# A sandwich of attention and routed low-rank layer: another order of VectorE's work in the middle of a pass

## The chip, the cores and the metric

The kernel runs on one core of one Trainium2 chip. The metric is the device time of one execution in microseconds (us); before the change it is 150.67 us, the median of 3 runs (150.66 to 150.72).

## What is computed

The input x has 16 sequences of 256 rows of 128 numbers, all fp32. Two residual sub-layers follow each other, each as x + layernorm(f(layernorm(x))):

```
def reference(x, ...):
    x = x + layernorm(attention(layernorm(x)))
    x = x + layernorm(ffn(layernorm(x)))

attention: 2 heads of 64; the upper 32 of each head's q and k are rotated (rotary angles);
           softmax(q k^T / 8) v, then the output projection Wo
ffn:       base = x W^T
           p = l2norm(x Wp^T + bp); logits = p @ l2norm(sim) * exp(min(temp, log 100))
           lw = softmax(logits); only the top expert of a row keeps its weight
           result = base + sum over experts e of lw_e * (x Wd_e^T) Wu_e^T,  ranks 1, 2, 4, 8
```

## The kernel before

**Tiling and stages.** The 16 sequences are worked as 8 pairs. A pair has 4 tiles of 128 rows (two per sequence) and 4 units (sequence b, head h: unit u = 2b + h). The kernel is one software pipeline written out by hand: the loop `for a in PASSES` (a = 0 to 6) stands once on each of four engines, and in pass a each engine does its share for several pairs at once: the attention of pair a, the projection of q, k and v of pair a + 1, the statistics of the first layernorm of pair a + 3, the residual after attention and its statistics for pair a - 1, and routing, gates and the final residual of pair a - 2. Pair 7 and the rest of pairs 5 and 6 are done after the loop in a written-out tail. Every engine executes its instructions in the order of the text; semaphores say when a value of another engine (or a small one of its own) is there. Nothing plans this order but the text.

**TensorE (PE), in one pass:** transposes of q and k (`turn_qk`, L1341), `project_qkv` (L1329 to L1331), transposes of the probabilities (`turn_probs`, L1362) and products with v (`weigh`, L1372) for units 0 to 3, `scores` (L1352), transposes of the gates (`turn_gated`, L1403), `low_rank` (L1410), and late in the pass `turn_x2` (L1383: transposes of the residual x after attention; it waits for all four tiles of `residual_y`), `turn_probs` of unit 3, `turn_qk` and `weigh` of unit 2, `project_z` (L1395), `turn_x` (L1322: transposes of the normalised x of pair a + 2, for which `normalise` of ACT and of DVE must be done).

**ScalarE (ACT):** the exponentials `exps` (L438, waits for the row maximum), copies from PSUM (`probs_copy`, `qk_copy`, `v_copy`, `qkt_copy`, `x2_copy`, `rows_up`, `gated_copy`), the sums of squares `variance_y` (L449) and `variance_z` (L474), half of `normalise` (L415) and `expert_exps` (L463, the exponentials of the routing, which wait for `logits`).

**GpSimd (POOL):** powers of four values per partition (`inverse_lengths` L293, `factors_y` L297, `norm_rows` L266, `factors_z` L305, `deviation` L309), and the rotation of q and k, `rope` (L282, L285, L288), three operations on 256 elements per partition with two SBUF inputs each, twice in a pass.

**VectorE (DVE)**, whose order the change rewrites: `row_max` (L675, negated row maxima of a unit's scores, read from PSUM); `weights_sum` and `add_head` (L680, L688); the first layernorm's statistics of pair a + 3: `stats` (L643, four times), `gap` (L649, L650), `mean` (L654, L655), `variance` (L659); the residual `residual_y` (L695, one tile each; inputs y_all and x_all, both in SBUF), its statistics `stats_2`, `gap_2`, `square_2`, `variance_2`; the routing chain `keys`, `top_key`, `logits`, `is_top`, `shares`, `pick`, `sum_exps`, `invert_sum`, `gates`, `gates_low` (L750 to L794), at whose end stands `gated`, which `turn_gated` transposes; `residual_z` (L799); `normalise` for tiles 0 and 1 of pair a + 2 (L664, SBUF to SBUF).

`logits` reads `below` and so far needs no wait of its own for it, as `keys`, which waits for it, stands in front. Passes 2, 3 and 4 have every part; pass 0 has no pair a - 1 or a - 2 and pass 1 no pair a - 2; in passes 5 and 6 there is no pair a + 3, so no `stats`, `gap`, `mean` or `variance`.

Of the kernel before, what the change touches and what calls it, by code (L numbers as in the profile page):

```python
# [43 lines left out]
def layer(nc, x, w_attn, vectors, w_ffn, w_down, sim, out):  # L44
# [3 lines left out]
    with ctx:  # L48
# [144 lines left out]
        def has(n):  # L193
            return 0 <= n < PAIRS
# [194 lines left out]
        def _(act):  # L389
# [56 lines left out]
            def variance_y(n, b):  # L446
                act.wait_ge(y_ready, n * 4 + 2 * b + 2)
                for t in (2 * b, 2 * b + 1):
                    last = act.activation(sq_y[:, t, :], y_all[:, n * PT + t, :], ACT.Square, scale=E ** -0.5,  # L449
                                          accum_out=var_y[:, t:t + 1])  # L450
                last.then_inc(vary, 1)
# [9 lines left out]
            def expert_exps(n):  # L461
                act.wait_ge(logits_ready, n + 1)
                act.activation(expl[:, :, :], logit[:, :, :], ACT.Exp).then_inc(exps_ready, 1)  # L463
# [62 lines left out]
            for a in PASSES:  # L526
                now, nxt, done = has(a), has(a + 1), has(a - 2)
                if done:
                    squares(a - 2)
                if now:  # L530
                    exps(a, 0)
                if a == 0:
                    rows_up(1)
                    v_first(0)
                    v_first(1)
                if now:
                    qkt_copy(a, 1)
                if has(a - 1):
                    variance_y(a - 1, 1)
                if now:  # L540
                    exps(a, 1)
                if done:
                    expert_exps(a - 2)
                if now:
                    probs_copy(a, 0)
                if nxt:
                    qk_copy(a + 1, 0)
                    v_copy(a + 1, 0)
                    qk_copy(a + 1, 1)
                    v_copy(a + 1, 1)  # L550
                    qk_copy(a + 1, 2)
                if now:
                    probs_copy(a, 1)
                if done:
                    gated_copy(a - 2)
                if nxt:
                    v_copy(a + 1, 2)
                if now:
                    exps(a, 2)
                if done:  # L560
                    variance_z(a - 2)
                if now:
                    exps(a, 3)
                if nxt:
                    qk_copy(a + 1, 3)
                if now:
                    probs_copy(a, 2)
                if has(a - 1):
                    x2_copy(a - 1)
                if has(a + 2):  # L570
                    act.wait_ge(rstd1, a + 1)
                    normalise(a + 2)
                if now:
                    variance_y(a, 0)
                if nxt:
                    qkt_copy(a + 1, 0)
                if now:
                    probs_copy(a, 3)
                if has(a + 2):
                    rows_up(a + 2)  # L580
                if nxt:
                    v_copy(a + 1, 3)
# [34 lines left out]
        def _(dve):  # L617
# [112 lines left out]
            def rank_wide(row):  # L730
                return row[:, :].unsqueeze(2).to_broadcast([P, PT, RANK])
# [18 lines left out]
            def keys(n):  # L750
                dve.wait_ge(route_link, n * 9 + 3)
                dve.scalar_tensor_tensor(key[:, :, :], below[:, :, :], 0.0,
                                         code[:, :].unsqueeze(1).to_broadcast([P, PT, RANK]), ALU.is_ge, ALU.mult).then_inc(route_link, 1)
# [4 lines left out]

            def logits(n):
                dve.wait_ge(inv_norm_ready, n + 1)  # L760
                dve.tensor_tensor(logit[:, :, :], below[:, :, :], rank_wide(inv_norm), ALU.mult).then_inc(logits_ready, 1)

            def is_top(n):
# [304 lines left out]
            for a in PASSES:  # L1068
                now, nxt, far, last_, done = has(a), has(a + 1), has(a + 2), has(a - 1), has(a - 2)
                if done:  # L1070
                    add_bias(a - 2, 1)
                if nxt and a >= 1:
                    rows_low(a + 1)
                if done:
                    top_logit(a - 2)
                    square_sum(a - 2)
                if now:
                    row_max(a, 0)
                if done:
                    length(a - 2)  # L1080
                if last_:
                    weights_sum(a - 1, 3)
                if done:
                    below_top(a - 2)
                if last_:
                    add_head(a - 1, 3, 0)
                    add_head(a - 1, 3, 1)
                if now:
                    row_max(a, 1)
                if a == 0:  # L1090
                    rows_low(1)
                    centre_bias()
                    later_weights(1)
                    for t in range(PT):
                        stats(2, t)
                    gap(2)
                    mean(2)
                    variance(2)
                if a == 1:
                    later_weights(5)  # L1100
                if done:
                    keys(a - 2)
                if has(a + 3):
                    stats(a + 3, 0)
                if done:
                    top_key(a - 2)
                    logits(a - 2)
                    is_top(a - 2)
                if has(a + 3):
                    stats(a + 3, 1)  # L1110
                    stats(a + 3, 2)
                if done:
                    shares(a - 2)
                    pick(a - 2)
                if has(a + 3):
                    stats(a + 3, 3)
                if done:
                    sum_exps(a - 2)
                if last_:
                    residual_y(a - 1, 0)  # L1120
                if done:
                    invert_sum(a - 2)
                if has(a + 3):
                    gap(a + 3)
                if done:
                    gates(a - 2)
                if has(a + 3):
                    mean(a + 3)
                if done:
                    gates_low(a - 2)  # L1130
                if has(a + 3):
                    variance(a + 3)
                if now:
                    row_max(a, 2)
                if last_:
                    residual_y(a - 1, 1)
                    residual_y(a - 1, 2)
                if now:
                    row_max(a, 3)
                    weights_sum(a, 0)  # L1140
                if a == 0:
                    later_weights(3)
                if last_:
                    stats_2(a - 1, 0)
                if now:
                    add_head(a, 0, 0)
                if last_:
                    stats_2(a - 1, 1)
                if now:
                    add_head(a, 0, 1)  # L1150
                if last_:
                    residual_y(a - 1, 3)
                    stats_2(a - 1, 2)
                    stats_2(a - 1, 3)
                if now:
                    weights_sum(a, 1)
                if last_:
                    gap_2(a - 1)
                if now:
                    add_head(a, 1, 0)  # L1160
                if last_:
                    square_2(a - 1)
                if now:
                    add_head(a, 1, 1)
                if last_:
                    variance_2(a - 1)
                if done:
                    residual_z(a - 2, 0)
                    residual_z(a - 2, 1)
                if far:  # L1170
                    normalise(a + 2)
                if done:
                    residual_z(a - 2, 2)
                    residual_z(a - 2, 3)
                if now:
                    weights_sum(a, 2)
                if a == 0:
                    later_weights(2)
                if last_:
                    scaled_bias(a - 1)  # L1180
                if now:
                    add_head(a, 2, 0)
                if last_:
                    add_bias(a - 1, 0)
                if now:
                    add_head(a, 2, 1)
                if a == 0:
                    later_weights(4)
# [436 lines left out]
```

## Time and profile before

| what | us |
|---|---|
| median of 3 runs | 150.67 |
| the profiled execution | 150.58 |
| its span in the profile | 148.8 |
| PE busy | 128.5 (86%) |
| DVE busy | 130.7 (88%) |
| ACT busy | 113.4 (76%) |
| POOL busy | 87.3 (59%) |

The profiled execution's own time is 1.8 us above its span (start and end outside of the profile) and 0.09 us below the median. "Busy" is the share of the span in which an engine had an instruction under way. The granted TensorE clock is 9 tenths or more of full speed in 37 of the 40 slices of the page and lower only in the last three, after the loop. Line numbers (L654) are those of the kernel before. In the lists over time, an instruction's duration runs from its start to its end, and the next one on the same engine may start some 0.08 us before that end; in the chain of waits each piece is counted from the end of the piece before it.

### The profile page before, as it was taken

The page shows a single profiled execution, that of the slowest core. Times are in us where ns is not written, and L with a number is a line of the kernel's source. Part 1 is how long each engine was busy: PE and PEld are TensorE (multiplying, and loading weights), DVE is VectorE, ACT ScalarE, POOL GpSimd, SP SyncE. Part 2 cuts the span into 40 slices and gives each one's busy share as a digit, 9 for nine tenths or more (in the row PEclk, how much of TensorE's full clock was granted, in tenths as well). Part 3 has the DMA queues.
Part 4 walks back from the last instruction along what each step waited for, and adds up shares of the span by engine and source line. Part 5 has one row for each costly group of instructions (what it writes and reads, how often), then busy time and mean ns, then how long its engine had stood idle before and what let it go on. Part 6 is the DMA issues. An engine that isn't in the chain of part 4 may idle for free.

```text
span 148.8 us, 3110 instructions
## 1 busy us (share of the span) xinstructions
PE 128.5 (86%) x874; PEld 106.0 (71%) x874; DVE 130.7 (88%) x592; ACT 113.4 (76%) x378; POOL 87.3 (59%) x148
## 2 busy tenths in 40 slices
PE   0879799999999998999899989998999898965340
PEld 0467587988898788878887888797879776953220
DVE  6788879997988999899989998898889788899963
ACT  3657697969996989698969896989698958754460
POOL 6320826623846758676867686768545863338552
PEclk9999999999999999999999999999999999999555
DMA  3833250000000000100020002000200010000013
GB/s 74 209 98 92 74 134 5 4 0 0 7 0 2 0 0 4 70 0 2 4 73 0 0 0 75 0 0 0 73 4 2 9 62 0 4 0 2 0 70 141
DMA packets 5266, 4.83 MB, mean 32 GB/s; under 512 B 594, under 2 KB 5250, under 8 KB 5250
## 3 DMA queue, kind: packets, MB, share of 16 engines
q1 hardware_dynamic: 5104, 4.51, 10.4%
q8 instruction: 7, 0.11, 0.3%
q10 hardware_dynamic: 146, 0.13, 0.3%
q14 instruction: 9, 0.07, 0.2%
HBM read 2.54 MB, written 2.10 MB: 31 GB/s over the span
## 4 chain that ended last, share of the span: by engine, by line
PE 49%; DVE 27%; ACT 15%; issue 2%; POOL 2%; DMA 2%; POOLq 1%; DVEq 0%
PE ps_a L1372 6%; PE ps_s L1352 6%; ACT probs L438 6%; PE ps_z L1395 5%; PE ps_c L1372 4%; DVE neg_max L675 4%; PE ps_a L1362 4%; DVE x_all L695 3%; PE ps_b L1322 2%; PE ps_s L1383 2%; PE ps_s L1341 2%; PE ps_b L1362 2%; DVE y_all L688 2%; DMA x_all<-x 2%; PE ps_c L1341 2%
## 5 line engine op out<-in xcount | busy, mean ns | idle before, releaser
L438 ACT ACTIVATE probs<-ps_s,neg_max 128x256 f32<-128x256 f32 x60 | 25.3, 488 | 7.9 <-DVE neg_max L675 7.8
L675 DVE TENSOR_REDUCE neg_max<-ps_s 128x2 f32<-128x512 f32 x30 | 20.3, 680 | 0.6 <-PE ps_s L1352 0.4
L1352 PE MATMUL ps_s<-qk_t 64*128 64x256 f32 x120 | 17.0, 402 | 0.0
L1372 PE MATMUL ps_a<-v_all,probs_t 128*128 128x129 f32 x120 | 16.5, 280 | 0.0
L1372 PEld LDWEIGHTS ps_a<-v_all,probs_t 128*128 128x128 f32 x120 | 14.6, 191 | 2.0 <-issue 2.0
L1352 PEld LDWEIGHTS ps_s<-qk_t 64*128 64x128 f32 x120 | 10.3, 186 | 4.8 <-issue 4.0
L282 POOL TENSOR_TENSOR turn<-qk,sin_x 128x256 f32<-128x256 f32 x15 | 11.1, 740 | 3.1 <-ACT qk L424 2.2
L695 DVE SCALAR_TENSOR_TENSOR x_all<-y_all,rsy,x_all 128x128 f32<-128x128 f32 x32 | 11.8, 393 | 1.3 <-POOL rsy L297 0.7
L285 POOL TENSOR_TENSOR qk<-qk,cos_x 128x256 f32<-128x256 f32 x15 | 11.5, 767 | 1.2
L297 POOL TENSOR_TENSOR rsy<-var_y,power 128x4 f32<-128x4 f32 x6 | 6.5, 1078 | 9.3 <-ACT sq_y L449 9.3
L293 POOL TENSOR_TENSOR inv_norm<-norm,power 128x4 f32<-128x4 f32 x7 | 7.2, 1027 | 8.0 <-DVE norm L744 8.0
L288 POOL TENSOR_TENSOR qk<-qk,turn 128x256 f32<-128x256 f32 x15 | 10.9, 725 | 1.2
L266 POOL TENSOR_TENSOR rs<-ve,power 128x4 f32<-128x4 f32 x7 | 7.1, 1008 | 6.2 <-DVE ve L659 6.2
L449 ACT ACTIVATE sq_y<-y_all 128x129 f32<-128x129 f32 x32 | 10.1, 339 | 0.7 <-DVE y_all L688 0.6
L309 POOL TENSOR_TENSOR std<-ve,root 128x4 f32<-128x4 f32 x7 | 7.1, 1017 | 5.3 <-DVE ve L716 5.3
L1362 PE MATMUL ps_a<-ident,probs 128*128 128x128 f32 x60 | 9.1, 275 | 1.1 <-ACT probs L438 1.1
L444 ACT ACTIVATE probs_t<-ps_a 128x512 f32<-128x512 f32 x15 | 9.5, 637 | 0.5 <-PE ps_a L1362 0.5
L1395 PE MATMUL ps_z<-w_z,x_t 128*128 128x190 f32 x48 | 9.5, 325 | 0.0
L1362 PEld LDWEIGHTS ps_a<-ident,probs 128*128 128x128 f32 x60 | 7.0, 140 | 2.6 <-ACT probs L438 1.6
L1372 PE MATMUL ps_c<-v_all,probs_t 128*128 128x129 f32 x64 | 8.6, 278 | 0.2 <-ACT probs_t L444 0.2
L799 DVE SCALAR_TENSOR_TENSOR x_all<-ps_z,rsz,x_all 128x128 f32<-128x128 f32 x24 | 7.3, 342 | 1.4 <-POOL rsz L305 1.4
L1372 PE MATMUL ps_b<-v_all,probs_t 128*128 128x129 f32 x64 | 8.5, 276 | 0.0
(342 smaller groups left out, 442.0 us busy)
## 6 DMA issues: line engine op xcount, KB each, us to landing
x_all<-x SPq DMA_DIRECT2D x7, 256.0 KB, 2.8
out<-x_all SPq DMA_DIRECT2D x7, 256.0 KB, 2.1
x_all<-x SPq DMA_DIRECT2D x2, 128.0 KB, 2.7
out<-x_all SPq DMA_DIRECT2D x2, 128.0 KB, 1.7
w_raw<-w_attn ACTq DMA_DIRECT2D x1, 128.0 KB, 2.8
w_raw<-w_attn SPq DMA_DIRECT2D x1, 128.0 KB, 2.9
bo_bp<-vectors SPq DMA_DIRECT2D x1, 80.0 KB, 3.5
ffn_raw<-w_ffn SPq DMA_DIRECT2D x1, 71.5 KB
```

The costliest lines, as they stand in the source:

```text
L282: pool.tensor_tensor(turn[:, b, :, :, :], swapped, sin_x[:, :, :, :, :].rearrange("p t g h i -> p (t g) h i"), ALU.mult).then_inc(rope_mid, 1)
L285: pool.tensor_tensor(spatial, spatial, cos_x[:, :, :, :, :].rearrange("p t g h i -> p (t g) (h i)"), ALU.mult).then_inc(rope_mid, 1)
L288: pool.tensor_tensor(spatial, spatial, turn[:, b, :, :, :].rearrange("p g h i -> p g (h i)"), ALU.add).then_inc(rope_done, 1)
L438: last = act.activation(probs[:, u, j, :], scores_of(n, u)[:, j * T:(j + 1) * T], ACT.Exp, bias=neg_max[:, u, j:j + 1])
L444: act.activation(probs_t[:, u, :, :], unit_of(n, u)[:, :].rearrange("p (a t) -> p a t", a=TILES), ACT.Copy).then_inc(pt_out, 1)
L449: last = act.activation(sq_y[:, t, :], y_all[:, n * PT + t, :], ACT.Square, scale=E ** -0.5, accum_out=var_y[:, t:t + 1])
L675: dve.tensor_reduce(neg_max[:, u, :], scores_of(n, u)[:, :].rearrange("p (j k) -> p j k", j=TILES), AX.X, ALU.max, negate=True).then_inc(m ...
L695: dve.scalar_tensor_tensor(x_all[:, rows(n, t)], y_all[:, n * PT + t, 0:E], rsy[:, t:t + 1], x_all[:, rows(n, t)], ALU.mult, ALU.add).then ...
L1352: last = pe.matmul(scores_of(n, 2 * b + h)[:, j * T:(j + 1) * T], qk_t[r, b, 0, j * P:(j + 1) * P], qk_t[r, b, 1, :], start=True, stop=True)
L1362: last = pe.transpose(unit_of(n, u)[:, i * T + j * P:i * T + (j + 1) * P], probs[:, u, j, i * P:(i + 1) * P], ident[:, :])
L1372: last = pe.matmul(unit_of(n, u)[:, j * VW:(j + 1) * VW], probs_t[:, u, i, j * P:(j + 1) * P], v_all[:, at:at + VW], start=(i == 0), stop= ...
L1395: last = pe.matmul(z_of(n, k)[:, t, :], x2_t[:, 2 * k + t, :], w_z[:, :], start=(t == 0), stop=False, skip_group_check=True)
```

## The change

On DVE, `logits` moves in front of `keys` and gets a wait of its own for `below`. The four `stats` are spread otherwise between the parts of the routing chain, and the routing chain runs to its end (`gates_low`) with `residual_y` of tile 0 and `gap` in between. `mean` and `variance` leave the middle of the pass and stand behind `variance_2`, in front of `residual_z`. `residual_y` of tile 3 moves from behind `add_head(a, 0, 1)` to directly behind tiles 1 and 2, in front of `row_max(a, 3)`. On ACT, `expert_exps` moves in front of `exps(a, 1)`. PE, POOL and the DMA queues keep their order, and no instruction is added or removed besides the one wait.

```diff
--- before.py
+++ after.py
@@ -537,10 +537,10 @@
                     qkt_copy(a, 1)
                 if has(a - 1):
                     variance_y(a - 1, 1)
+                if done:
+                    expert_exps(a - 2)
                 if now:
                     exps(a, 1)
-                if done:
-                    expert_exps(a - 2)
                 if now:
                     probs_copy(a, 0)
                 if nxt:
@@ -758,6 +758,7 @@
 
             def logits(n):
                 dve.wait_ge(inv_norm_ready, n + 1)
+                dve.wait_ge(route_link, n * 9 + 3)
                 dve.tensor_tensor(logit[:, :, :], below[:, :, :], rank_wide(inv_norm), ALU.mult).then_inc(logits_ready, 1)
 
             def is_top(n):
@@ -1099,42 +1100,40 @@
                 if a == 1:
                     later_weights(5)
                 if done:
+                    logits(a - 2)
                     keys(a - 2)
                 if has(a + 3):
                     stats(a + 3, 0)
                 if done:
                     top_key(a - 2)
-                    logits(a - 2)
-                    is_top(a - 2)
                 if has(a + 3):
                     stats(a + 3, 1)
+                if done:
+                    is_top(a - 2)
+                    shares(a - 2)
+                if has(a + 3):
                     stats(a + 3, 2)
                 if done:
-                    shares(a - 2)
                     pick(a - 2)
+                    sum_exps(a - 2)
                 if has(a + 3):
                     stats(a + 3, 3)
                 if done:
-                    sum_exps(a - 2)
+                    invert_sum(a - 2)
                 if last_:
                     residual_y(a - 1, 0)
                 if done:
-                    invert_sum(a - 2)
+                    gates(a - 2)
                 if has(a + 3):
                     gap(a + 3)
                 if done:
-                    gates(a - 2)
-                if has(a + 3):
-                    mean(a + 3)
-                if done:
                     gates_low(a - 2)
-                if has(a + 3):
-                    variance(a + 3)
                 if now:
                     row_max(a, 2)
                 if last_:
                     residual_y(a - 1, 1)
                     residual_y(a - 1, 2)
+                    residual_y(a - 1, 3)
                 if now:
                     row_max(a, 3)
                     weights_sum(a, 0)
@@ -1149,7 +1148,6 @@
                 if now:
                     add_head(a, 0, 1)
                 if last_:
-                    residual_y(a - 1, 3)
                     stats_2(a - 1, 2)
                     stats_2(a - 1, 3)
                 if now:
@@ -1164,6 +1162,9 @@
                     add_head(a, 1, 1)
                 if last_:
                     variance_2(a - 1)
+                if has(a + 3):
+                    mean(a + 3)
+                    variance(a + 3)
                 if done:
                     residual_z(a - 2, 0)
                     residual_z(a - 2, 1)
```

## Rows read from the trace of the kernel before

**Rows 1.** Busy time by window; one window is one pass; us, then each engine's.

```profile
60.41:75.32 14.91, 14.30 (x106) 12.18 (x105) 14.43 (x62) 12.96 (x46) 10.62 (x17) 1.00 0.06 19
90.22:105.06 14.84, 14.29 (x106) 12.17 (x105) 12.85 (x53) 12.90 (x46) 10.80 (x17) 1.00 0.06 22
31.27:45.49 14.22, 14.19 (x103) 12.08 (x102) 12.62 (x50) 12.19 (x37) 7.12 (x11) 1.00 0.01 2
```

**Rows 2.** Chain of waits in pass 3: start, length, what.

```profile
71.24 0.66 PE ps_s L1383 x4
71.89 0.44 PE ps_a L1362 x4
```

**Rows 3.** DVE over time in pass 3, and L654 over the run (min/median/max).

```profile
66.62 0.73 DVE L654 SCALAR_TENSOR_TENSOR mean<-tmp,stats 128x4 f32<-128x4 f32 x1
67.47 0.69 DVE L659 SCALAR_TENSOR_TENSOR ve<-tmp 128x4 f32<-128x4 f32 x1
...
L654 DVE SCALAR_TENSOR_TENSOR mean<-tmp,stats x7: 165/168/726, 14.3 to 81.5; 128x4 f32<-128x4 f32 x7
```

**Rows 4.** POOL over time in pass 3.

```profile
66.59 0.74 POOL L282 TENSOR_TENSOR turn<-qk,sin_x 128x256 f32<-128x256 f32 x1
67.40 0.74 POOL L285 TENSOR_TENSOR qk<-qk,cos_x 128x256 f32<-128x256 f32 x1
```

**Rows 5.** Chain of waits in pass 5: start, length, what.

```profile
98.21 0.38 ACT gated_t L467
...
101.41 0.66 PE ps_a L1362 x4
```

**Rows 6.** ACT over time in pass 3.

```profile
64.21 0.84 ACT L438 ACTIVATE probs<-ps_s,neg_max 128x256 f32<-128x256 f32 x2
64.93 0.27 ACT L463 ACTIVATE expl<-logit 128x60 f32<-128x60 f32 x1
...
70.65 0.89 ACT L438 ACTIVATE probs<-ps_s,neg_max 128x256 f32<-128x256 f32 x2
```

**Rows 7.** PE's weight loads over time in pass 3.

```profile
65.52 0.73 PEld L1352 LDWEIGHTS ps_s<-qk_t 64*128 64x128 f32 x8 [0.36 <-issue]
```

**Rows 8.** DVE over time in pass 0.

```profile
26.58 0.16 DVE L680 RECIPROCAL den<-ps_a 128x2 f32<-128x2 f32 x1
...
28.66 1.38 DVE L664 TENSOR_SCALAR xn<-x_all,rs,nm 128x128 f32<-128x128 f32 x2
```

**Rows 9.** POOL over time in pass 0.

```profile
28.41 0.74 POOL L282 TENSOR_TENSOR turn<-qk,sin_x 128x256 f32<-128x256 f32 x1 [1.09 <-ACT qk L424]
...
30.04 0.72 POOL L288 TENSOR_TENSOR qk<-qk,turn 128x256 f32<-128x256 f32 x1
```

**Rows 10.** Chain of waits in passes 0 and 1: start, length, what.

```profile
25.43 0.89 PE ps_a L1372 x8
...
30.75 0.59 PE ps_b L1322 x4
...
41.41 0.66 PE ps_s L1383 x4
```

**Rows 11.** ACT over time in pass 1.

```profile
35.60 0.84 ACT L438 ACTIVATE probs<-ps_s,neg_max 128x256 f32<-128x256 f32 x2
```

**Rows 12.** PE over time in pass 1.

```profile
36.68 1.13 PE L1352 MATMUL ps_s<-qk_t 64*128 64x256 f32 x8
```

**Rows 13.** DVE over time in pass 1.

```profile
37.84 0.69 DVE L675 TENSOR_REDUCE neg_max<-ps_s 128x2 f32<-128x512 f32 x1
38.45 1.08 DVE L695 SCALAR_TENSOR_TENSOR x_all<-y_all,rsy,x_all 128x128 f32<-128x128 f32 x2
39.45 0.68 DVE L675 TENSOR_REDUCE neg_max<-ps_s 128x2 f32<-128x512 f32 x1
```

**Rows 14.** POOL over time in pass 1.

```profile
38.64 0.74 POOL L285 TENSOR_TENSOR qk<-qk,cos_x 128x256 f32<-128x256 f32 x1
39.46 0.72 POOL L288 TENSOR_TENSOR qk<-qk,turn 128x256 f32<-128x256 f32 x1
```

## Prediction

> **What bounds the kernel now.** I read the busy times by pass first. A full pass takes 14.91 us, and PE is busy for 14.30 us of it, DVE for 14.43 us [rows 1]. Both look full, so I asked which one waits. The chain of waits shows PE standing still at one place in a full pass: `turn_x2` starts at 71.24 us, when the last `residual_y` releases it, and takes 0.66 us where four transposes without a wait (the next row) take 0.44 [rows 2]. So DVE decides there, by about 14.91 - 14.30 = 0.6 us in each of passes 2 to 4, and PE decides elsewhere.
>
> Next, DVE's own list. `mean` and `variance` handle four elements per partition, yet take 0.73 and 0.69 us [rows 3]; the quickest `mean` of the run takes 0.165. The two end almost with POOL's L282 and L285 (67.35 against 67.33, 68.16 against 68.14) [rows 3, 4]: a DVE instruction with two SBUF inputs that comes while a `rope` operation runs stands until it is nearly over. That is 0.56 + 0.53 = 1.1 us of standing in each of three passes.
>
> **A pass that shows what comes next.** Pass 5 has no `stats`, `mean` or `variance`; DVE is busy for only 12.85 us in it, and `turn_x2` doesn't wait. Yet it takes 14.84 us, 0.07 less than pass 3 [rows 1]. There the chain goes through ACT: from `gated_copy` at 98.21 without a break to PE's `turn_probs` of unit 3 at 101.41, which waits for the last exponentials and takes 0.66 [rows 5]. `gated_copy` follows PE's own order, not DVE's gates.
>
> **The change, part by part.** The sum is made against the profiled execution's 150.58 us, 0.09 below the median of 150.67. A measurement of this kernel tells about 0.2% (0.3 us) from no change.
>
> *Mean and variance at the end, passes 2 to 4.* At their new place only POOL's powers run. DVE has 1.1 us less of standing, and the residual is done before PE asks for it. The naive sum is 3 x 0.6 = 1.8 us. But ACT's chain is next, as in pass 5, so I take 3 x 0.07 = -0.21 us. Bounds: 0 and -1.8; pass 5 is the nearest row, being the same pass with this DVE work gone.
>
> *Residuals of tiles 1 to 3.* They have two SBUF inputs too, and now reach the same `rope`. In pass 1 two of them take 1.08 us for some 0.6 [rows 13], as L285 runs until 39.38 [rows 14]. In passes 2 to 4 I expect DVE to reach `row_max(a, 2)` near 66.7 and the residuals at 67.3, to stand for one or two `rope` operations, and `row_max(a, 3)` to end near 69.8. ACT takes that unit at 70.65 [rows 6], so the cover is 0.8 us: cost 0. In passes 5 and 6 the same cover holds: 0. `add_head` and what follows start up to 0.6 us later there, beside a DVE wait for `factors_z` later in the pass: 0.
>
> *Pass 1.* `row_max(1, 2)` starts at 37.84 on the scores' end (36.68 + 1.13 = 37.81) [rows 12, 13], so moving `mean` away doesn't advance it. Tile 3 is now issued at 39.45, where L288 starts at 39.46 [rows 13, 14]: a tie. If it gets in, `turn_x2`, which starts at 41.41 after a wait and takes 0.66 [rows 10], gains 0.03 + 0.22 = 0.25 us. If it loses, it stands 0.6 us, and `row_max(1, 3)` begins 0.85 us late (0.6 and its own 0.26); the exponentials then end about when `turn_probs` needs them: 0, or up to +0.23 if the delay of the opening (next) has moved `rope` as well. I take 0 for the middle and keep -0.25 and +0.23.
>
> *Pass 0.* This is where the change may cost. Here `mean` and `variance` come directly before `normalise` of DVE, which begins at 28.66 just behind the start of a `rope` (L282 at 28.41, L288 at 30.04, L285 between them) [rows 8, 9] and already takes 1.38 us for two instructions. PE takes its result at once (30.75, no gap before it) [rows 10]. `row_max(0, 2)` and `(0, 3)` can go earlier, but DVE then waits for `weigh`, whose end at 25.43 + 0.89 = 26.32 lets L680 start near 26.37 instead of 26.58 [rows 8, 10]. So DVE reaches `mean` at 28.66 - 0.21 = 28.45, behind L282's start by 0.04 us, as in pass 3 (0.03, blocked). `mean` stands until about 29.0, `variance` meets L285 and stands until 29.8, the first `normalise` slips in, the second stands behind L288 (30.76) and ends near 30.9. `turn_x` then ends about 31.6 instead of 31.34: +0.25 us. DVE itself is 0.56 us late, contiguous into pass 1, so exponentials of unit 1 end at 36.44 + 0.56 = 37.0 [rows 11] while PE, late by 0.25, wants them at 36.93 [rows 12]: +0.11. PE has no idle time to absorb it (14.19 of 14.22 us busy) [rows 1]. Together +0.36 us; bounds 0 (the instructions miss the `rope`) and +0.6 (one more `rope` operation stands in the way).
>
> *Expert exponentials first on ACT.* `logits` ends when ACT would start `exps(a, 1)` (64.21 [rows 6]), so ACT waits some 0.05 us, then runs `expert_exps`, 0.15 us net. The unit's exponentials end at 64.21 + 0.84 + 0.2 = 65.25; PE loads for the next scores at 65.52 [rows 6, 7]: cover 0.27, cost 0. DVE's wait for `shares` goes, where nobody waited. If the cover is gone, up to 0.1 us in each of passes 2 to 6. The added wait of `logits` is for a value long there: 0, with nothing queued behind it late.
>
> *Gates earlier.* `turn_gated` stands in PE's queue behind `weigh(a, 0)` and found its gates ready: 0.
>
> **Sum:** -0.21 + 0.36 + 0 = +0.15 us; 150.58 + 0.15 = 150.73, on the scale of the median 150.82 us.
>
> **What the skill says.** The Trainium skill, "VectorE: DVE Perf Modes", section on the DRAIN one can't avoid, has each DVE instruction wait for the pipe of the one before, whatever the order, and counsels to reduce their count. By that alone a reordering is neutral and the sum is 150.58; the trace disagrees with it as a whole account (0.165 against 0.726 us for the same instruction). The Trainium skill, "GPSIMD Engine Reference", section Specifications, says GpSimd's SBUF interfaces are shared with VectorE, with contention for DVE instructions with two SBUF inputs or in a 2-port mode. That speaks against this change: it holds for the residuals and `normalise` as for `mean`. The trace agrees (1.08 and 1.38 us for two).
>
> **Rivals.**
> - *Faster* (0.22). The opening misses the `rope`, and in pass 1 tile 3 gets in: -0.21 - 0.25 = -0.46, 150.2 on the median's scale. For it: ties of 0.01 to 0.04 us decide both. Against: `mean` at +0.03 was blocked three times. If ACT's chain also shortened, up to -1.8; nothing shows how.
> - *Slower* (0.28). One mechanism: DVE's instructions with two inputs fall behind every operation of `rope` in passes 0 and 1. Opening +0.36, and in pass 1 tiles 1, 2 and 3 each stand, `row_max(1, 3)` ends after 41.5, and the exponentials come 0.23 us late to PE: +0.36 + 0.23 - 0.21 = +0.38, 151.05. It decides from the point where `row_max(1, 3)` ends later than 1.5 us before `turn_probs` of unit 3.
> - *Order is neutral* (0.08, within "same"): the standing only changes places and nothing reaches PE: 150.67.
>
> **How the numbers follow.** Likeliest (0.42): opening pays, passes 2 to 4 give back, 150.82. With the neutral case, "same" has 0.50, faster 0.22, slower 0.28. The range goes from about the faster case's 150.2 (150.3, leaving its tail out) to the slower case's 151.05 plus 0.24 for the opening's upper bound: 150.3 to 151.3.
>
> **What would show it.** Right: `mean` and `variance` at 0.17 us in passes 1 to 4, but long in pass 0; one or more `residual_y` of 0.8 us in each pass; no PE wait at `turn_x2` in passes 2 to 4, one of about 0.5 us for the exponentials before `turn_probs` of unit 3; passes 2 to 4 of 14.84 us; `turn_x` of pass 0 0.2 to 0.3 us later. Wrong: passes clearly under 14.84 us (ACT wasn't next), a wait before `scores` for exponentials of unit 1 (the swap on ACT costs), or an unchanged opening.

## The result, and the profile after

The changed kernel takes 151.78 us (median of 4 runs, 151.76 to 151.9) against 150.69 us for the kernel before (150.66 to 150.76): ratio 1.0074, 95% interval 1.0063 to 1.0086, some 1.1 us slower. I had forecast 150.82 with a range of 150.3 to 151.3. The profiled execution took 151.90 us with a span of 150.1. Medians are of undisturbed executions; the only other one, of g_vz_norm (316.4 us), is left out. The one added line is L761, and most of what stands behind it is one line lower in the text, so PE's L1383 is now L1384 and DVE's L799 is L800; the experiments' kernels are shifted by a few lines likewise.

The first view is the busy time by pass, as in [rows 1]: pass 3, then pass 5 (window, length, then the busy time of PE, PE's weight loads, DVE, ACT and POOL).

```profile
61.47:76.46 14.99, 14.46 (x106) 12.15 (x105) 14.75 (x64) 13.02 (x47) 10.42 (x17) 1.00 0.06 19
91.46:106.29 14.83, 14.28 (x105) 12.16 (x104) 13.76 (x55) 12.87 (x46) 10.27 (x17) 1.00 0.08 28
```

Pass 5 is as before, but pass 3 went from 14.91 to 14.99 where I expected 14.84, and DVE, with 1.1 us of standing taken out of its middle, is busy for longer (14.75 against 14.43). The standing has changed places. PE over time in pass 2 shows that the old wait is gone and the one I had forecast is there:

```profile
56.53 0.60 PE L1384 MATMUL ps_s<-ident,x_all 128*128 128x128 f32 x4
57.66 0.66 PE L1363 MATMUL ps_a<-ident,probs 128*128 128x128 f32 x4 [0.54 <-ACT probs L438]
```

**Where the rest of a pass goes** is told by DVE over time, in the middle and at the end of pass 3:

```profile
67.74 0.69 DVE L675 TENSOR_REDUCE neg_max<-ps_s 128x2 f32<-128x512 f32 x1
68.35 1.88 DVE L695 SCALAR_TENSOR_TENSOR x_all<-y_all,rsy,x_all 128x128 f32<-128x128 f32 x3
70.15 0.68 DVE L675 TENSOR_REDUCE neg_max<-ps_s 128x2 f32<-128x512 f32 x1
...
73.04 0.16 DVE L654 SCALAR_TENSOR_TENSOR mean<-tmp,stats 128x4 f32<-128x4 f32 x1
...
73.91 1.13 DVE L664 TENSOR_SCALAR xn<-x_all,rs,nm 128x128 f32<-128x128 f32 x2
```

and by POOL over time at the same place (`factors_z`, `deviation`, then the second `rope` of the pass):

```profile
72.23 1.04 POOL L305 TENSOR_TENSOR rsz<-var_z,power 128x4 f32<-128x4 f32 x1
73.25 1.04 POOL L309 TENSOR_TENSOR std<-ve,root 128x4 f32<-128x4 f32 x1
74.23 0.73 POOL L282 TENSOR_TENSOR turn<-qk,sin_x 128x256 f32<-128x256 f32 x1
```

`mean` is down to 0.16 us, as forecast, and the residuals meet `rope` instead (1.88 us for three), which is covered. But two `normalise` now take 1.13 us. In the kernel before they take 0.59, and the `rope` comes later (DVE, then POOL, pass 3):

```profile
72.95 0.59 DVE L664 TENSOR_SCALAR xn<-x_all,rs,nm 128x128 f32<-128x128 f32 x2
```

```profile
73.58 0.72 POOL L282 TENSOR_TENSOR turn<-qk,sin_x 128x256 f32<-128x256 f32 x1
```

DVE's statistics of the residual are done 0.45 us earlier in the pass, so POOL's `deviation` follows `factors_z` without a wait, and the second `rope` starts at 74.23 - 61.47 = 12.8 us into the pass, 0.4 us earlier than before (13.2). `normalise` starts only 0.1 us earlier (12.44 us into the pass for 12.54), since `mean` and `variance` now stand in front of it, three instructions that take DVE 0.35 us. So the `rope` catches the second `normalise`. The last `residual_z` is late, and `project_z` waits for it: its last four products take 0.77 us in the chain of waits (pass 2), where the first four take 0.65.

```profile
59.65 0.65 PE ps_z L1396 x4
60.30 0.47 PE ps_b L1323 x4
60.77 0.77 PE ps_z L1396 x4
```

**Pass 0** lost what was forecast, 0.27 us, by nearly the forecast way. DVE over time, then PE:

```profile
28.94 0.50 DVE L654 SCALAR_TENSOR_TENSOR mean<-tmp,stats 128x4 f32<-128x4 f32 x1
29.36 0.15 DVE L655 SCALAR_TENSOR_TENSOR tmp<-tmp 128x4 f32<-128x4 f32 x1
29.55 0.70 DVE L659 SCALAR_TENSOR_TENSOR ve<-tmp 128x4 f32<-128x4 f32 x1
30.17 1.00 DVE L664 TENSOR_SCALAR xn<-x_all,rs,nm 128x128 f32<-128x128 f32 x2
```

```profile
31.23 0.65 PE L1323 MATMUL ps_b<-ident,xn 128*128 128x128 f32 x4 [0.22 <-DVE xn L664]
```

I had put `mean` 0.04 us behind the start of L282; it is 0.26 us behind it (28.94 against 28.68). DVE was 0.2 us early at L680, but lost that again in a stand that I had overlooked, behind the `rope` operation L288 of the first sequence. DVE over time, in the kernel before and in the changed one:

```profile
26.65 0.23 DVE L958 TENSOR_TENSOR sim_n<-sim_raw,sim_n 32x4 f32<-32x4 f32 x1
```

```profile
26.72 0.44 DVE L959 TENSOR_TENSOR sim_n<-sim_raw,sim_n 32x4 f32<-32x4 f32 x1
```

**Pass 1** is bound by DVE. Its chain of waits, beside [rows 10, 13]:

```profile
39.25 1.90 DVE x_all L695 x3
41.15 0.60 DVE neg_max L675
...
42.47 0.26 DVE y_all L688
42.73 0.14 issue
42.87 0.63 PE ps_a L1363 x4
```

`turn_probs` of unit 3 waits for two things, the exponentials of unit 3 and the bank that `add_head` of unit 0 reads. Both stand behind `row_max(1, 3)`. The exponentials end at 42.63, `add_head` at 42.72, so the latter releases PE, by 0.09 us.

Counted between the starts of PE's `scores` (in pass 0 from `turn_probs` of unit 3), the stretches stand so, in us:

| stretch | before | after |
|---|---|---|
| pass 0, `turn_probs` to `scores` of pair 1, first sequence | 3.08 | 3.35 |
| from there to `scores` of its second sequence | 5.41 | 5.61 |
| from there to the start of pass 2 | 8.81 | 9.06 |
| passes 2, 3, 4 | 14.92, 14.91, 14.90 | 14.99, 14.99, 15.00 |
| pass 5 | 14.84 | 14.83 |

The differences are 0.27, 0.20, 0.25 and (passes 2 to 4 together) 0.25: 0.97 us of the 1.09 between the medians. The profiled execution is also 0.27 us late before pass 0's `turn_probs`, in work that the change doesn't touch; other kernels' profiles below vary there by as much, so I don't count it.

### The profile page after: what moved, and what is told of

Its sections match the earlier page's. It is cut to its first block, busy times and chain, and to the rows that moved or that the text cites. A ratio compares the mean times of both kernels' runs of the same rounds, so it can differ in the third digit from the quotient of the medians.

```text
span 150.1 us, 3117 instructions
## 1 busy us (share of the span) xinstructions
PE 129.8 (86%) x874; PEld 106.5 (71%) x874; DVE 134.2 (89%) x592; ACT 113.2 (75%) x378; POOL 86.6 (58%) x148
## 4 chain that ended last, share of the span: by engine, by line
PE 57%; DVE 18%; ACT 15%; issue 3%; POOL 2%; DMA 2%; POOLq 1%; DVEq 0%
PE ps_s L1353 10%; PE ps_a L1373 9%; ACT probs L438 6%; PE ps_z L1396 5%; PE ps_a L1363 5%; PE ps_c L1373 4%; ACT sq_z L474 3%; PE ps_b L1363 3%; PE ps_c L1342 3%; PE ps_b L1323 2%; DVE y_all L688 2%; DMA x_all<-x 2%; PE ps_s L1342 2%; DVE x_all L695 2%; ACT gated_t L467 1%
## 5 line engine op out<-in xcount | busy, mean ns | idle before, releaser
L1353 PE MATMUL ps_s<-qk_t 64*128 64x256 f32 x120 | 17.6, 412 | 0.1
L695 DVE SCALAR_TENSOR_TENSOR x_all<-y_all,rsy,x_all 128x128 f32<-128x128 f32 x32 | 15.8, 535 | 1.2 <-POOL rsy L297 0.7
L1353 PEld LDWEIGHTS ps_s<-qk_t 64*128 64x128 f32 x120 | 10.8, 193 | 5.2 <-issue 4.4
L282 POOL TENSOR_TENSOR turn<-qk,sin_x 128x256 f32<-128x256 f32 x15 | 11.1, 737 | 3.7 <-ACT qk L424 3.1
L285 POOL TENSOR_TENSOR qk<-qk,cos_x 128x256 f32<-128x256 f32 x15 | 11.5, 764 | 1.2
L288 POOL TENSOR_TENSOR qk<-qk,turn 128x256 f32<-128x256 f32 x15 | 11.1, 740 | 1.2
L1373 PEld LDWEIGHTS ps_c<-v_all,probs_t 128*128 128x128 f32 x64 | 7.8, 191 | 0.5 <-ACT probs_t L444 0.4
```

Source lines behind the costliest of these rows:

```text
L282: pool.tensor_tensor(turn[:, b, :, :, :], swapped, sin_x[:, :, :, :, :].rearrange("p t g h i -> p (t g) h i"), ALU.mult).then_inc(rope_mid, 1)
L285: pool.tensor_tensor(spatial, spatial, cos_x[:, :, :, :, :].rearrange("p t g h i -> p (t g) (h i)"), ALU.mult).then_inc(rope_mid, 1)
L288: pool.tensor_tensor(spatial, spatial, turn[:, b, :, :, :].rearrange("p g h i -> p g (h i)"), ALU.add).then_inc(rope_done, 1)
L695: dve.scalar_tensor_tensor(x_all[:, rows(n, t)], y_all[:, n * PT + t, 0:E], rsy[:, t:t + 1], x_all[:, rows(n, t)], ALU.mult, ALU.add).then ...
L1353: last = pe.matmul(scores_of(n, 2 * b + h)[:, j * T:(j + 1) * T], qk_t[r, b, 0, j * P:(j + 1) * P], qk_t[r, b, 1, :], start=True, stop=True)
L1373: last = pe.matmul(unit_of(n, u)[:, j * VW:(j + 1) * VW], probs_t[:, u, i, j * P:(j + 1) * P], v_all[:, at:at + VW], start=(i == 0), stop= ...
```

## The experiments

Each was timed in 5 rounds beside the kernel before on the same chip. Ratios are to the kernel before, whose median was 150.69 to 150.72 us beside every one of them; differences from the changed kernel are taken between medians, without an interval of their own. "A" stands for the theory that DVE's instructions meeting `rope` make up the loss.

**One part at a time: mean and variance (m_only).** On the kernel before:

```diff
-                if has(a + 3):
-                    mean(a + 3)
                 if done:
                     gates_low(a - 2)
-                if has(a + 3):
-                    variance(a + 3)
...
                     variance_2(a - 1)
+                if has(a + 3):
+                    mean(a + 3)
+                    variance(a + 3)
```

> Kernel before with only mean and variance moved behind variance_2. Theory A (DVE's two-input instructions meet POOL's rope): the loss of pass 0 comes with this part alone, turn_x of pass 0 about 0.3 us late and the scores of unit 1 in pass 1 some 0.2 us more; pass 1 adds nothing, as tile 3's residual stands where it stood; in passes 2 to 4 rope of the second sequence starts earlier against the pass and catches normalise, so these passes are 14.9 us or more. Sum +0.4 to +0.8 us over before. Rival B (the loss lies with the routing chain and the swap on ACT): no slower than before, -0.2 to 0. Rival C (start-up scatter only): same as before.

Measured 151.94 us, ratio 1.0083 (1.0070 to 1.0097): this part alone costs more than the whole change, and more than the +0.4 to +0.8 us that A had (+1.25). Pass 0 has the same stand (`normalise` 1.00 us, PE waiting). Passes 2 to 4 take 15.12, 15.14 and 15.14 us, and the last stretch of pass 1 8.90 us (+0.09). With the old routing order another instruction meets `rope` in `mean`'s place, so DVE is later on the way to the end of the pass (`normalise` starts 0.19 us later in it than in the changed kernel), and there `normalise` is caught too. DVE over time, pass 3:

```profile
67.66 0.67 DVE L794 TENSOR_TENSOR gated<-gate,gated 128x60 fp32r<-128x60 f32 x1
...
73.94 1.09 DVE L664 TENSOR_SCALAR xn<-x_all,rs,nm 128x128 f32<-128x128 f32 x2
```

`gated` takes 0.67 us for the 0.21 that it takes elsewhere. B and C fall.

**Tile 3's residual (r_only).** On the kernel before:

```diff
                     residual_y(a - 1, 2)
+                    residual_y(a - 1, 3)
                 if now:
                     row_max(a, 3)
...
-                    residual_y(a - 1, 3)
```

> Kernel before with only tile 3's residual moved in front of row_max(a, 3). Theory A: in pass 1 it stands behind the third rope operation, row_max(1, 3) is about 0.85 us late, and turn_probs of unit 3 waits: 0 to +0.25 us there; in passes 2 to 4 turn_x2 no longer waits and they take 14.84 instead of 14.91: -0.2. Sum -0.2 to +0.1 us. Rival B: 0.

Measured 150.59 us, ratio 0.9997 (0.9988 to 1.0006). The last stretch of pass 1 takes 8.99 us for 8.81 (+0.18), passes 2 to 4 take 14.82, 14.83 and 14.83 (-0.25 in all): both as A has it, and together no difference that can be told.

**Routing chain and swap on ACT (g_only).** The changed kernel with its two moves undone:

```diff
                     gates_low(a - 2)
+                if has(a + 3):
+                    mean(a + 3)
+                    variance(a + 3)
                 if now:
                     row_max(a, 2)
...
-                    residual_y(a - 1, 3)
...
+                    residual_y(a - 1, 3)
                     stats_2(a - 1, 2)
...
-                if has(a + 3):
-                    mean(a + 3)
-                    variance(a + 3)
```

> The change without its two moves: routing chain, spread of stats and the swap on ACT as changed, mean and variance in the middle directly in front of row_max(a, 2), tile 3's residual where it was. Theory A: nobody waited for the gates and the swap is covered by 0.2 us: 0 +- 0.2 us against before; mean and variance still take 0.7 us. Rival B: +0.5 to +1.1 us, with PE waiting for the exponentials of unit 1.

Measured 150.52 us, ratio 0.9989 (0.9981 to 0.9998). The swap costs nothing. Passes 2 to 4 take 14.82 to 14.84 us. One detail went otherwise than expected: `mean` and `variance` are 0.15 and 0.16 us here, since only the small instruction between them (L655) comes behind the start of `rope`:

```profile
66.61 0.15 DVE L654 SCALAR_TENSOR_TENSOR mean<-tmp,stats 128x4 f32<-128x4 f32 x1
66.69 0.73 DVE L655 SCALAR_TENSOR_TENSOR tmp<-tmp 128x4 f32<-128x4 f32 x1
67.45 0.16 DVE L659 SCALAR_TENSOR_TENSOR ve<-tmp 128x4 f32<-128x4 f32 x1
```

```profile
66.63 0.78 POOL L282 TENSOR_TENSOR turn<-qk,sin_x 128x256 f32<-128x256 f32 x1 [0.21 <-ACT qk L424]
67.48 0.73 POOL L285 TENSOR_TENSOR qk<-qk,cos_x 128x256 f32<-128x256 f32 x1
```

One stand instead of two: the first instruction starts 0.02 us before L282 and gets through, the next one stands, and the third slips in before L285. So DVE reaches `row_max(a, 2)` 0.5 us earlier in the pass. Half of it and more is lost again, as two residuals now take 1.08 us for 0.67, and PE still waits for tile 3, though less than before (0.47 for 0.61 us). PE over time, pass 3:

```profile
71.10 0.66 PE L1384 MATMUL ps_s<-ident,x_all 128*128 128x128 f32 x4 [0.47 <-DVE x_all L695]
```

`turn_probs` of unit 3 follows at 11.19 us into the pass, the place that ACT's exponentials allow in r_only too: here DVE and ACT come out level, to some 0.02 us.

**The opening undone (open_mid).** On the changed kernel, `mean` and `variance` of pass 0 alone go back to the middle:

```diff
+                if a == 0:
+                    mean(a + 3)
+                    variance(a + 3)
                 if now:
                     row_max(a, 2)
...
-                if has(a + 3):
+                if a >= 1 and has(a + 3):
                     mean(a + 3)
```

> The changed kernel with mean and variance of pass 0 alone back in the middle. Theory A: turn_x of pass 0 no longer waits, normalise in pass 0 takes 1.4 us again, row_max to exponentials in pass 1 are back: 0.4 to 0.6 us faster than the changed kernel, +0.5 to +0.7 over before. Rival B: as slow as the changed kernel (+1.1).

Measured 151.15 us, ratio 1.0033 (1.0020 to 1.0045): 0.63 us less than the changed kernel. `turn_x` of pass 0 doesn't wait. The stretches are 3.07, 5.43 and 8.99 us, so the opening was worth 0.28 + 0.18 + 0.07 = 0.53 us in the trace. Pass 3 of this profile took 14.84 us, passes 2 and 4 14.98, so a part of the 0.63 can be that; it is told at the end.

**And pass 1 undone (open_mid_t3).** Added to that run:

```diff
+                if a >= 2:
                     residual_y(a - 1, 3)
                 if now:
                     row_max(a, 3)
...
+                if a == 1:
+                    residual_y(a - 1, 3)
```

> The changed kernel with mean and variance of pass 0 back in the middle and tile 3's residual of pass 1 at its old place. Theory A: pass 1's scores-to-scores distance goes back from 8.99 to 8.81 us: 0.15 to 0.2 us faster than the run with mean and variance alone back (151.15), so near 150.95; passes 2 to 4 stay at 14.84 to 15.0. Rival D (the loss of pass 1 comes from the lateness of the opening alone): as that run, 151.15.

Measured 151.01 us, ratio 1.0019 (1.0010 to 1.0028). The stretch is 8.82 us again, and passes 2 to 4 are 14.99, 15.00 and 14.99. D falls: tile 3's residual in front of `row_max(1, 3)` costs its 0.17 us by itself.

**Normalise in front (norm_first).** On the changed kernel:

```diff
-                if done:
-                    residual_z(a - 2, 0)
-                    residual_z(a - 2, 1)
                 if far:
                     normalise(a + 2)
                 if done:
+                    residual_z(a - 2, 0)
+                    residual_z(a - 2, 1)
                     residual_z(a - 2, 2)
```

> The changed kernel with DVE's normalise in front of residual_z of tiles 0 and 1. Theory A (in passes 2 to 4 rope of the second sequence starts earlier against the pass and catches the second normalise): both normalise end before that rope, take 0.6 us together again, and passes 2 to 4 take 14.84 us instead of 14.99: 0.3 to 0.45 us faster than the changed kernel, near 151.4. Rival E (the extra 0.15 us is mean and variance themselves, late on DVE): passes stay at 14.99, 151.8.

Measured 151.72 us, ratio 1.0069 (1.0056 to 1.0081): no gain, and a miss. The stand is gone (`normalise` takes 0.59 us for two), but the passes take 15.01 us, as now the first two `residual_z` are late for the first `project_z`. DVE over time, then the chain of waits, pass 3:

```profile
73.08 0.59 DVE L664 TENSOR_SCALAR xn<-x_all,rs,nm 128x128 f32<-128x128 f32 x2
73.60 1.12 DVE L800 SCALAR_TENSOR_TENSOR x_all<-ps_z,rsz,x_all 128x128 f32<-128x128 f32 x4
```

```profile
74.33 0.83 PE ps_z L1395 x4
75.16 0.44 PE ps_b L1322 x4
75.60 0.65 PE ps_z L1395 x4
```

By itself this run decides nothing: E's result for another reason. The next one decides.

**The late rope held (late_rope_held).** On the changed kernel, DVE as it is, POOL waits:

```diff
+                if 2 <= a <= 4:
+                    pool.wait_ge(out_ready, 4 * (a - 2) + 4)
                 if has(a + 1):
                     rope(a + 1, 1)
```

> The changed kernel with POOL's second rope of passes 2 to 4 held until all four residual_z of the pass are done (a wait added on POOL, nothing else). Theory A: normalise takes 0.6 us for two, project_z gets its banks in time, passes 2 to 4 take 14.84 us: 0.3 to 0.45 us faster than the changed kernel, unless rope, now some 0.6 us later, comes too late for turn_qk of the second sequence, which starts 2 us into the next pass. Rival E: no change, 151.8, or slower by the held rope.

Measured 151.18 us, ratio 1.0032 (1.0020 to 1.0045): 0.60 us less than the changed kernel. DVE's order is untouched, yet two `normalise` take 0.59 us and passes 2 to 4 take 14.83, 14.84 and 14.83. DVE over time, then POOL, pass 3:

```profile
73.44 0.59 DVE L666 TENSOR_SCALAR xn<-x_all,rs,nm 128x128 f32<-128x128 f32 x2
```

```profile
74.63 0.91 POOL L282 TENSOR_TENSOR turn<-qk,sin_x 128x256 f32<-128x256 f32 x1 [0.82 <-DVE x_all L802]
```

E falls as it was put: `mean` and `variance` cost these passes nothing by themselves. The passes give 0.48 of the 0.60 us; the other 0.12 I can't place.

**The early rope held, in the kernel before (rope_held).**

```diff
+                if 2 <= a and has(a + 3):
+                    pool.wait_ge(var1, a + 3)
                 if has(a + 1):
                     rope(a + 1, 0)
```

> The kernel before with POOL's first rope of passes 2 to 4 held until DVE's variance is done (a wait added on POOL, nothing else). Theory A (a rope operation holds up a DVE instruction with two SBUF inputs): mean and variance take 0.17 us each in passes 2 to 4, but the residuals behind meet rope in their place; turn_x2 waits less or not at all, and the passes take 14.84 to 14.91 us: -0.2 to 0 us. Rival F (mean is slow at that place for another reason, as its inputs or PE's or ACT's traffic): it still takes 0.7 us.

Measured 150.48 us, ratio 0.9983 (0.9974 to 0.9992): the fastest of all these kernels, by about what can be told from no change. The same DVE code as in [rows 3], and the same place:

```profile
66.69 0.15 DVE L656 SCALAR_TENSOR_TENSOR mean<-tmp,stats 128x4 f32<-128x4 f32 x1
...
66.84 0.21 DVE L796 TENSOR_TENSOR gated<-gate,gated 128x60 fp32r<-128x60 f32 x1
66.97 0.15 DVE L661 SCALAR_TENSOR_TENSOR ve<-tmp 128x4 f32<-128x4 f32 x1
```

F falls: `mean` goes from 0.73 to 0.15 us when `rope` isn't there (it starts at 67.20). The two residuals behind take 1.24 us for 0.67, and passes 2 to 4 take 14.84, 14.83 and 14.83, with PE waiting for the exponentials of unit 3.

This run shows something more. Its second `rope` starts 12.73 us into the pass, as early as in the changed kernel (12.77), and the two `normalise` take 0.59 us all the same: they start at 12.34 us, without `mean` and `variance` in front of them, for 12.44 there. The early `rope` does no harm alone; it takes `mean` and `variance` in front of `normalise` as well. Pass 5, which has neither, shows the same in the kernel before. DVE over time, then POOL:

```profile
102.57 0.60 DVE L664 TENSOR_SCALAR xn<-x_all,rs,nm 128x128 f32<-128x128 f32 x2
```

```profile
102.95 0.80 POOL L282 TENSOR_TENSOR turn<-qk,sin_x 128x256 f32<-128x256 f32 x1
```

There `normalise` starts 0.38 us before the `rope`, against 0.63 us in pass 3 of that kernel and 0.32 us in the changed one.

**All three repairs (all_held).** open_mid_t3 and the wait of late_rope_held together.

> The changed kernel with all three repairs: mean and variance of pass 0 in the middle, tile 3's residual of pass 1 at its old place, and POOL's second rope held until residual_z is done in passes 2 to 4. Theory A (three places make up the whole loss): 151.01 - 0.45 = near 150.5 us, 0.1 to 0.3 us faster than before, as the first sum had it for passes 2 to 4 (3 x 0.07) and no more. Rival G (a loss is left elsewhere): 150.8 or more.

Measured 150.57 us, ratio 0.9991 (0.9982 to 1.0000): 1.21 us less than the changed kernel. G falls; the three places make up the loss. Against the kernel before, the gain is at the edge of what can be told.

**What bounds a pass of 14.83 us: variance_z later.** Three runs put ACT's `variance_z` behind the exponentials of unit 3, on g_only (g_vz_late), on the kernel before (before_vz_late) and on g_vz_late with `normalise` in front as in norm_first (g_vz_norm):

```diff
                 if now:
                     exps(a, 2)
+                    exps(a, 3)
                 if done:
                     variance_z(a - 2)
-                if now:
-                    exps(a, 3)
```

> Routing chain and swap alone (150.52), with ACT's variance_z of passes 2 to 6 behind the exponentials of unit 3. Theory A (ACT's stretch from gated_copy to those exponentials is what bounds a pass of 14.83 us): turn_probs of unit 3 no longer waits for it; up to 0.5 us a pass less, but residual_z comes 0.75 us later, and project_z needs its banks: between -0.5 us a pass and +0.3, the wait before turn_probs gone in either case. Rival H (something else bounds a pass): the passes stay at 14.83.

> The kernel before with only ACT's variance_z behind the exponentials of unit 3. Theory A: passes 2 to 4 are bound by DVE's residual of tile 3 there, so nothing is gained in them (0, or a loss where residual_z comes late), passes 5 and 6, bound by ACT, gain or lose as in the run with the routing chain changed. Rival H: no change anywhere.

> As the run of the routing chain and late variance_z, and DVE's normalise in front of residual_z of tiles 0 and 1, so that turn_x does not wait behind residual_z. Theory A: DVE works on normalise while POOL's rsz is late; passes no longer than in that run, up to 0.3 us shorter. Rival: project_z of tiles 0 and 1 waits for residual_z all the same, and nothing is gained.

Measured 152.86 (1.0146, 1.0132 to 1.0160), 153.24 (1.0171, 1.0157 to 1.0185) and 152.92 us (1.0146, 1.0131 to 1.0162). All lose, and the first by more than the bound I had set for A: its passes take 15.34 us, which is +0.51. In its chain of waits ACT's sums of squares are followed by POOL, DVE and then PE:

```profile
71.34 1.04 ACT sq_z L474 x8
...
72.77 1.03 POOL rsz L305
73.82 0.62 DVE x_all L799 x2
...
74.49 0.91 PE ps_z L1395 x4
```

A late `variance_z` holds `project_z` back. In pass 5 of this run `turn_probs` of unit 3 starts 10.48 us into the pass instead of 11.19, so it is the exponentials that it had waited for; in passes 2 to 4 it stays at 11.17, behind DVE's residual. Both ends of ACT's stretch thus have someone waiting: the exponentials, and behind the variance the banks of `project_z`. The runs don't show what a pass would take with the stretch shortened, as these builds still have tile 3's residual at its late place; that wasn't tried. No profile of g_vz_norm is read.

## Why the prediction was wrong, point by point

- *What bounds the kernel, and who follows.* Right. PE waited for DVE's residual in passes 2 to 4, and with that gone ACT bounds the pass at 14.83 us in r_only, rope_held, late_rope_held and all_held, as pass 5 had shown: `turn_probs` of unit 3 starts 11.18 to 11.20 us into the pass, though DVE's last residual ends anywhere from 8.8 to 10.2 us. (In g_only DVE and ACT are level.) The naive 1.8 us was never there; 0.25 was.
- *Mean and variance at the end, passes 2 to 4, taken at -0.21, bounds 0 and -1.8.* This is the step that failed, and its sign. "At their new place only POOL's powers run" was true of `mean` itself. But I followed DVE's gain only to PE. It also released POOL's `deviation` earlier, `rope` behind it started 0.4 us earlier against the pass, `mean` and `variance` kept `normalise` from moving as much, and the second `normalise` stood. Measured +0.25 us, and late_rope_held takes it back. My bound of 0 excluded a loss without a reason. The model, pass 5, hid it: there `rope` is as early, but `mean` and `variance` don't exist, and `normalise` has 0.38 us on it. With both in front it has 0.32, and that isn't enough.
- *Pass 0, taken at +0.36, bounds 0 and +0.6.* Right in the mechanism: `mean` behind L282's start, `normalise` late, `turn_x` +0.27 (forecast 0.25), the second `scores` +0.20 (0.11). One reading was wrong: `mean` was no tie of 0.04 us, since L959 had stood first. It was mis-sized: 0.53 by the trace (0.07 of it in the last stretch of pass 1, which the sum had at 0), 0.63 by the medians.
- *Pass 1, taken at 0, bounds -0.25 and +0.23.* The size lay in the bounds: +0.18 by r_only, +0.25 with the late opening. The link was half right: the exponentials of unit 3 do come late for `turn_probs`, but `add_head`, which I hadn't priced for this pass, comes 0.09 us later still and releases it.
- *Residuals of passes 2 to 6, gates, swap on ACT, at 0 each.* Nobody waits, as forecast: three residuals take 1.88 us, and `row_max(a, 3)` ends within 0.1 us of the forecast place; g_only has no wait before `scores`. But the routing order isn't at 0: it takes one of the two stands out, and passes 2 to 4 are 0.23 us shorter in g_only.
- *The slower rival* had the mechanism and 151.05 us with a chance of 0.28. It missed the third place, the end of passes 2 to 4: it counted -0.21 us for them, and they cost +0.25.

The rule of the Trainium skill, "GPSIMD Engine Reference", section Specifications, that speaks of contention for two SBUF inputs or a 2-port mode, agrees with the stands in these traces: `mean`, `variance`, the residuals and `gated`, with two SBUF inputs, stand; `row_max` and `residual_z`, which read PSUM, don't (0.69 us and 0.59 us for two beside `rope`). `normalise` has one SBUF input besides its factors, and no run here shows whether it runs in a 2-port mode. The rule doesn't tell which POOL operations count: the powers have two SBUF inputs as well, and `mean` takes 0.16 us beside one.

## What to carry to other kernels

Taking an instruction out of a stand behind another engine's long operation doesn't by itself remove the stand; in the runs here the next instructions with two SBUF inputs took over some or all of it, and their consumer decides the price. When an engine gets faster, follow whom it releases as well as who waits for it: here an earlier `deviation` moved a `rope` of 2.4 us onto `normalise`. A pass that serves as a model must also be asked what it lacks and how much room its meetings leave. Where such a meeting matters, try one wait that holds the long operation on its own engine (0.60 us back here) before rewriting the order of the other.

## What the runs showed of the hardware that I hadn't expected

Whether the second `normalise` gets through or stands turns on less than 0.1 us. From the start of the two `normalise` to L282 it is 0.38 to 0.40 us in 21 of the passes 2 to 5 of these profiles, and in all of them it got through; at 0.28 to 0.32 us it stood in 11 passes of 12. The twelfth shows that the profile's start times don't decide it. In open_mid the two `normalise` and L282 stand as follows in passes 2, 3 and 4 (DVE over time, then POOL):

```profile
58.27 1.13 DVE L664 TENSOR_SCALAR xn<-x_all,rs,nm 128x128 f32<-128x128 f32 x2
...
73.27 0.59 DVE L664 TENSOR_SCALAR xn<-x_all,rs,nm 128x128 f32<-128x128 f32 x2
...
88.09 1.13 DVE L664 TENSOR_SCALAR xn<-x_all,rs,nm 128x128 f32<-128x128 f32 x2
```

```profile
58.59 0.73 POOL L282 TENSOR_TENSOR turn<-qk,sin_x 128x256 f32<-128x256 f32 x1
...
73.59 0.86 POOL L282 TENSOR_TENSOR turn<-qk,sin_x 128x256 f32<-128x256 f32 x1
...
88.41 0.73 POOL L282 TENSOR_TENSOR turn<-qk,sin_x 128x256 f32<-128x256 f32 x1
```

The distance is 0.32 us each time, yet in pass 3 the second `normalise` (which starts some 0.07 us before L282) got through and POOL's operation took 0.13 us longer, while in the other two DVE stood for 0.54 us. Such passes differ by 0.14 us in one execution of one code. POOL's powers on four elements, 1.0 us long, held nothing up: in the changed kernel DVE's `gap` takes 0.15 us and `mean` 0.16 us beside one.
